# A state-space block with an FP4 feed-forward: the partial state and the output product from rounded halves

## The chip, the cores and the metric

The kernel runs on one core of one Trainium2 chip. The metric is the device time of one execution in microseconds (us); the median of three runs is shown. Five engines work side by side, each through its own instructions in order: TensorE (PE, matrix products and transposes into PSUM), VectorE (DVE), ScalarE (ACT), GpSimd (POOL), and SyncE (SP), which here only issues transfers. They wait for each other on semaphores.

## The reference, cut to what matters

The input is x of 8 x 2048 x 256 in float32. The first half is a simplified Mamba block, the second a feed-forward whose operands are quantised to FP4 in blocks of 16:

```
x_proj, z = split(x @ W_in)                      # 512 + 512 columns
x_conv = silu(causal 4-tap conv(x_proj) + conv_b)
ssm = x_conv @ W_xproj                           # 1 + 16 + 16 columns: delta, B, C
deltaB = softplus(ssm[..., 0]) * B
h_mean = einsum('bld,bln->bdn', x_conv, deltaB) / L      # the state
y = (einsum('bdn,bln->bld', h_mean, C) + D * x_conv) * silu(z)
x = layernorm(x + y @ W_out)                     # the output product
x = layernorm(x + fp4(silu(fp4(x) @ fp4(w_gate).T) * (fp4(x) @ fp4(w_up).T)) @ fp4(w_down).T)
```

## The kernel before, in words

The sequence is cut into 32 groups of 512 positions, four to a batch row. A group has four steps (j = 0 to 3), and a step works on a block of 128 of the 512 inner columns in the first half, and on a tile of 128 positions in the second. All stages run in one software pipeline, whose order is written out by hand for each engine. In one step of the steady part, group g, PE does in this order:

1. gate and up products of an earlier tile (`gate_and_up`, 18 products),
2. the input product of this block (`x_product`), and transposes of an earlier tile's FP4 values (`transposed_h`),
3. `y_product`: the finished state of a batch row times C, for a block five groups back. DVE adds the D term (`skip`, line 1128), POOL multiplies by silu(z) (line 460) into `g`,
4. `output_projection` (line 608): four products of `g` (128 x 128) with `wout` (128 x 256), both float32,
5. only in j = 2: `partial_state` (line 619), four products of `dB` (128 x 48) with `xct` (128 x 512), both float32, summed into bank pc; DVE adds pc into `hacc` (line 1134),
6. `state_projection` and `transposed_conv` of the block before (its transpose goes through bank pa into `xct`, which has two slots, one for each of two groups), `transposed_x`, `z_product`; in j = 3 also `transposed_c` (line 678), which uses bank pa again,
7. `down_projection`, 17 products of 256 columns.

In j = 2 the products of item 6 stand in another order than in the rest (`transposed_x`, `z_product`, `state_projection`, `transposed_conv`).

The other products are made of float32r halves already: a value is rounded to float32r (high), the rest to float32r as well (low), and high x high, high x low and low x high are summed (`split_product`, line 532).

`dB` is made by DVE in `scaled_b`, at the end of step j = 1 (lines 1138 and 1142), so it is ready a step before its use. DVE's order in a steady step is: the sum after the down product (line 1164), codes of x (1001 to 1013), two convolution taps (1104), rounding of x (1019, 1022), `h_product` (1190), `skip` (1128), `h_absmax` (1001), `h_rests` (1199, 1202), `h_scales` (1005, 1009), `attn_sum` (1218), `h_codes` (1013), `add_projection` (1115 or 1119), `x_rests` (1228), `h_round` (1019, 1022; the first waits for ACT's magnitudes, line 898), and in j = 2 at the end the split of the next input (`split_input`, line 1037).

POOL multiplies the values of x (427), gates (460), sums a tap (`conv_sum`, 450), does three small operations of the layer norm (411, 413, 415), and multiplies the codes of h (470, 472). ACT normalises with their result (`r1_rows`, line 904); after that, it makes in j = 0 the softplus (from line 808 on) and in j = 2 the high half of the next input (line 780). DVE's x codes of the next step read what `r1_rows` wrote. ACT's `x_big` (line 867) comes behind the softplus, and DVE's rounding of x waits for it.

The first 24 steps also quantise and transpose the weights; the last 20 have no first half any more.

Of the kernel before, what the change touches and what calls it, by code (L numbers as in the profile page):

```python
# [52 lines left out]
def block_kernel(nc, x, x_t, W_in, conv_w, conv_b, W_xproj, D_skip, W_out, w_gate, w_up, w_down, out):  # L53
# [13 lines left out]
    H3 = 3 * NS  # L67
    LAG = SPS + 1
# [11 lines left out]
    with ExitStack() as ctx:  # L80
# [13 lines left out]
        wout = sb("wout", [P, NB, DM])  # L94
# [11 lines left out]
        ctr = sb("ctr", [H3, SPS, ST], F32R)  # L106
# [9 lines left out]
        xct = sb("xct", [P, 2, TPS, DI])  # L116
# [4 lines left out]
        ccat = sb("ccat", [P, TPS, H3])  # L121
        hacc = sb("hacc", [H3, DI])
        hcat = sb("hcat", [H3, DI], F32R)

        g = sb("g", [P, 2, NB, ST])
# [58 lines left out]
        xct_copied = sem("xct_copied")  # L184
        ssm_pe = sem("ssm_pe")
# [16 lines left out]
        yd_done = sem("yd_done")  # L202
        g_ready = sem("g_ready")
        xres_landed = [sem("xres_landed0"), sem("xres_landed1")]
# [37 lines left out]
        scratch = sb("scratch", [P, 5 * GW + 2 * FF + KM * P])  # L242
        flat_g = g[:, :, :, :].rearrange("p a b c -> p (a b c)")
        raw_g = scratch[:, 0:GW]
        raw_u = flat_g[:, GW + 9 * (GW // QB):2 * GW + 9 * (GW // QB)]
        raw_d = scratch[:, 5 * GW:5 * GW + 2 * FF]
        twice_d = scratch[:, 5 * GW + 2 * FF:5 * GW + 2 * FF + KM * P]
        quant_w = [scratch[:, n * GW:(n + 1) * GW] for n in range(1, 4)]
        w_big = [scratch[:, 4 * GW:5 * GW], flat_g[:, 0:GW], raw_g]

        at = [0]

        def over_scratch(width):

            at[0] += width
            assert at[0] <= scratch.shape[1]
            return scratch[:, at[0] - width:at[0]]

# [8 lines left out]
        GQ = GW // QB  # L267
        w_small = [[flat_g[:, GW + (3 * n + r) * GQ:GW + (3 * n + r + 1) * GQ] for r in range(3)]
                   for n in range(3)]
# [45 lines left out]

        def conv_bank(g_):

            return pgu[:, 1024:1536] if g_ <= LAG else pa[:, :]

# [7 lines left out]
        def _(q):  # L327
# [19 lines left out]
            def body(g_, s, b):  # L347
                i = g_ - LAG
                for j in range(TPS):
# [6 lines left out]
                    if exists(w + 1):  # L356

                        n, half = (j + 1) % 2, 16 * (2 * i + (j + 1) // 2 + 1)
                        wait_apart(q, (xc_saved[n], half), (sz_saved[n], half), (g_ready, w))
                        q.dma_start(xl[:, n, :], xc_hbm[w + 1]).then_inc(xl_landed[n], 16)  # L360
                        q.dma_start(zl[:, n, :], sz_hbm[w + 1]).then_inc(zl_landed[n], 16)
# [22 lines left out]
        def _(pool):  # L384
# [33 lines left out]
            def body(g_, s, b):  # L418
                i = g_ - LAG
                for j in range(TPS):  # L420
# [35 lines left out]
                    if p2 and g_ <= NSUP:  # L456
# [3 lines left out]
                        pool.tensor_tensor(g[:, second(s) % 2, j, :], g[:, second(s) % 2, j, :], zl[:, j % 2, :],  # L460
                                           ALU.mult).then_inc(g_ready, 1)
                    if p1 and g_ > LAG:
                        conv_sum()
                    if exists(to) and g_ <= NSUP:
                        layer_norm(to, ssq1_done, r1_ready, rs1_eps, rs1_done, nm1_done, sum1, ssq1, rs1, nm1)
                    if exists(tg):
# [6 lines left out]
                                           spread(qsh[:, :, 1]), ALU.mult).then_inc(hprod_done, 1)  # L473
                    if j == 0 and exists(v):
# [3 lines left out]
                        c2 = ccat[:, :, :].rearrange("p t (a n) -> p t a n", a=3)  # L478
                        pool.tensor_copy(c2[:, :, 0, :].bitcast(F32R), c_in)
                        pool.tensor_copy(c2[:, :, 2, :].bitcast(F32R), c_in).then_inc(cc_hi, 1)  # L480
# [32 lines left out]
        def _(pe):  # L513
# [40 lines left out]

            def x_product(j, g_, u, v):
# [5 lines left out]
                if g_ > LAG:  # L561
                    at_least(pe, xct_copied, v)
# [13 lines left out]
            def y_product(j, s, b, g_, v, w):  # L576

                wait_apart(pe, (h_ready, b - 1 if s == 0 else b), (ct_ready, g_ - LAG + 1), (g_ready if g_ > NSUP else yd_done, w),
                           (ssm_added, capped(v, NT)))
                if j == 3 and g_ == LAG:  # L580
                    pe.wait_ge(h_added, g_)
# [13 lines left out]
            def output_projection(j, s, i, g_, to, tz):  # L595
# [8 lines left out]
                if i == 1 and j == 0:  # L604
                    pe.wait_ge(w_landed, 32)
                    pe.wait_ge(ct_ready, LAG)
                for c in range(NB):
                    mm = pe.matmul(bank[:, 0:DM], g[:, (second(s) + 1) % 2, c, j * P:(j + 1) * P],  # L608
                                   wout[:, c, :], start=(c == 0), stop=(c == NB - 1))
                mm.then_inc(o_pe, 1)  # L610

            def partial_state(n, added, w):
# [5 lines left out]
                for t in range(TPS):  # L618
                    mm = pe.matmul(pc[0:H3, :], dB[:, t, :], xct[:, (n - 1) % 2, t, :],
                                   start=(t == 0), stop=(t == TPS - 1))  # L620
                mm.then_inc(h_pe, 1)

            def state_projection(j, jb, g_, v, w):
# [6 lines left out]
                elif LAG - 1 <= g_ <= LAG and j == 3 or g_ > LAG and j == 2:  # L630
# [8 lines left out]
            def transposed_conv(g_, jb, u, v):  # L639

                pe.wait_ge(xc_ready, v + 1)
                if g_ <= LAG:
                    at_least(pe, xct_copied, v)
# [26 lines left out]
            def transposed_c(g_, v):  # L670
# [3 lines left out]
                else:  # L674
                    wait_apart(pe, (cc_ready, g_), (xct_copied, capped(v + 1, NT)))
                bank = c_bank(g_)
                for t in range(TPS):
                    mm = pe.transpose(bank[0:H3, t * P:(t + 1) * P], ccat[:, t, :], ident[:, :])
# [20 lines left out]
            def body(g_, s, b):  # L699
                i = g_ - LAG  # L700
                tail = exists(g_ - 1, NSUP)
                for j in range(TPS):
# [3 lines left out]
                    if g_ <= LAG:  # L706
# [5 lines left out]
                        if j == 1 and 2 <= g_ < LAG:  # L712
                            partial_state(g_ - 1, v, w)
                        if exists(v):
                            state_projection(j, jb, g_, v, w)
                            transposed_conv(g_, jb, u, v)
                        if j == 2 and LAG - 1 <= g_:
# [4 lines left out]
                    if g_ > NSUP:  # L722
# [4 lines left out]
                        if exists(td):  # L727
                            transposed_h(td, u)
                        if exists(to):
                            output_projection(j, s, i, g_, to, tz)  # L730
                        if p2:
                            skip_product(j, i, w)
# [17 lines left out]
                    if j == 2 and tail:  # L750
# [614 lines left out]
```

## Time and profile before

| | us |
|---|---|
| median of three runs (1985.72 to 1989.41) | 1985.98 |
| the profiled execution, whole | 1988.75 |
| its span, first to last instruction | 1987.0 |
| PE busy in the span | 1920.3 (97%) |
| DVE busy | 1578.8 (79%) |
| ACT busy | 1265.9 (64%) |
| POOL busy | 1102.5 (55%) |

The granted TensorE clock is 0.986 of full speed in the mean. An engine's busy time says how full it is, not whether the others wait for it. The records of successive products of PE overlap, so what a product costs is read from the distance between starts. Offsets into a step are counted from the start of its first gate product; in one steady group the steps j = 1, 2, 3, 0 start at 998.76, 1012.34, 1029.63 and 1043.62 us, and the next at 1057.20.

### The profile page before, as it was taken

Reading aid. Unit: us, or ns where it says so; the run is one execution under the profiler, and the core shown is the slowest. Engines: PE = TensorE matmul, PEld = TensorE weight load, DVE = VectorE, ACT = ScalarE, POOL = GpSimd, SP = SyncE. Lnnn points to the kernel's source line nnn. Section 1 sums busy time; section 2 is a strip of 40 time slices with the busy share of each in tenths; the row PEclk is TensorE's granted clock in tenths of the full one; section 3 lists DMA queues with packets and bytes.
Section 4 is the critical chain, followed back from the end, with each engine's and each line's share of the span. In section 5 each row is a group of like instructions: output and inputs, shape, how many; then the busy total and the mean of one; then the engine's idle time right before and its main releaser. Section 6 shows DMA issues by size and latency. Waiting matters only on the chain. (4 is left out here: it accounts for less than half of the span.)

```text
span 1987.0 us, 34279 instructions
## 1 busy us (share of the span) xinstructions
PE 1920.3 (97%) x10180; PEld 1540.1 (78%) x10180; DVE 1578.8 (79%) x3549; ACT 1265.9 (64%) x2617; POOL 1102.5 (55%) x1758
## 2 busy tenths in 40 slices
PE   6898999999999999999999999999999999999996
PEld 5665788888878888888788788888888888777775
DVE  5645788878888888888888888888788887788885
ACT  6776666666666666666666666666666666544443
POOL 3434555556555656655556665565565556555553
PEclk8898999999999999999999999999999999999998
DMA  5234233232322322323223232232323223222210
GB/s 167 96 122 144 91 100 103 89 109 99 102 100 98 99 95 99 109 94 109 96 85 107 99 109 96 99 104 88 109 99 101 100 88 99 69 65 73 72 38 16
DMA packets 120309, 190.60 MB, mean 96 GB/s; under 512 B 15040, under 2 KB 49728, under 8 KB 120128
## 3 DMA queue, kind: packets, MB, share of 16 engines
q1 hardware_dynamic: 120128, 188.42, 28.5%
q8 instruction: 85, 1.39, 0.3%
q14 instruction: 96, 0.79, 0.1%
HBM read 104.48 MB, written 83.89 MB: 95 GB/s over the span
## 5 line engine op out<-in xcount | busy, mean ns | idle before, releaser
L532 PE MATMUL pgu<-wgu_hi,xqT 128*128 128x512 f32 (+1 forms) x1536 | 427.1, 386 | 7.6 <-issue 6.5
L532 PEld LDWEIGHTS pgu<-wgu_hi,xqT 128*128 128x128 f32 x1536 | 278.7, 189 | 72.0 <-issue 9.9
L532 PE MATMUL pd<-wd_hi,hqT 128*128 128x256 f32 (+1 forms) x1536 | 315.9, 297 | 5.2 <-issue 2.1
L532 PEld LDWEIGHTS pd<-wd_hi,hqT 128*128 128x128 f32 (+1 forms) x1536 | 247.7, 190 | 26.6 <-issue 4.8
L1019 DVE SCALAR_TENSOR_TENSOR scratch<-scratch 128x256 f32<-128x256 f32 (+2 forms) x258 | 171.8, 666 | 96.7 <-ACT scratch L898 77.4
L411 POOL TENSOR_SCALAR rs<-ssq 128x1 f32<-128x1 f32 x256 | 72.4, 283 | 310.3 <-issue 297.3
L532 PE MATMUL pgu<-wgu_lo,xqT 128*128 128x512 f32 (+1 forms) x768 | 228.0, 378 | 0.0
L1104 DVE SCALAR_TENSOR_TENSOR acc<-xps,cw,acc 128x512 f32<-128x512 f32 x256 | 200.3, 782 | 30.8 <-POOL acc L450 26.2
L608 PE MATMUL pd<-wout,g 128*128 128x256 f32 x864 | 215.4, 392 | 0.0
L802 ACT ACTIVATE scratch<-scratch,sum 128x256 f32<-128x256 f32 x256 | 130.2, 509 | 123.4 <-DVE scratch L1164 118.4
L472 POOL TENSOR_TENSOR scratch<-hnq,qsh 128x704 f32<-128x704 bf16 x128 | 188.7, 1474 | 0.0
L608 PEld LDWEIGHTS pd<-wout,g 128*128 128x128 f32 x864 | 155.2, 189 | 42.6 <-issue 25.8
L413 POOL TENSOR_TENSOR rs<-rs,nhalf 128x1 f32<-128x1 f32 x256 | 170.4, 666 | 21.6
L532 PE MATMUL pd<-wd_lo,hqT 128*128 128x256 f32 x640 | 181.6, 284 | 0.0
L872 ACT ACTIVATE scratch<-pgu 128x704 f32<-128x704 f32 x128 | 96.6, 755 | 116.5 <-PE pgu L532 116.5
L450 POOL TENSOR_TENSOR acc<-acc,tap 128x512 f32<-128x512 f32 x128 | 164.3, 1284 | 11.4 <-ACT tap L846 11.4
L635 PEld LDWEIGHTS pc<-wxp,xcs 128*128 128x128 f32 x1024 | 134.6, 194 | 38.5 <-ACT xcs L829 21.6
L460 POOL TENSOR_TENSOR g<-g,early 128x512 f32<-128x512 f32 x112 | 143.1, 1278 | 35.5 <-DVE g L1128 35.2
L532 PEld LDWEIGHTS pgu<-wgu_lo,xqT 128*128 128x128 f32 x768 | 143.2, 189 | 23.5
L415 POOL TENSOR_SCALAR nm<-sum,rs 128x1 f32<-128x1 f32 x256 | 131.4, 513 | 43.8 <-POOL rs L413 43.8
L635 PE MATMUL pc<-wxp,xcs 128*128 128x33 f32 x1024 | 128.7, 271 | 24.6 <-ACT xcs L829 17.5
L427 POOL TENSOR_TENSOR scratch<-xnq,qsx 128x256 f32<-128x256 bf16 x128 | 81.3, 635 | 118.6 <-DVE xnq L1022 115.5
(140 smaller groups left out, 4489.8 us busy)
## 6 DMA issues: line engine op xcount, KB each, us to landing
sz_hbm<-szs SPq DMA_DIRECT2D x128, 256.0 KB, 2.0
xc_hbm<-xcs SPq DMA_DIRECT2D x128, 256.0 KB, 2.0
early<-xc_hbm SPq DMA_DIRECT2D x128, 256.0 KB, 2.7
early<-sz_hbm SPq DMA_DIRECT2D x128, 256.0 KB, 3.0
xin<-in_x_t_dram SPq DMA_DIRECT2D x32, 512.0 KB, 4.7
xres<-in_L_attn_x_dram SPq DMA_DIRECT2D x128, 128.0 KB, 2.4
out_dram<-scratch SPq DMA_DIRECT2D x128, 128.0 KB, 1.7
early<-in_L_attn_W_in_dram SPq DMA_DIRECT2D x2, 512.0 KB, 4.7
```

What stands on the lines that cost most here:

```text
L413: pool.tensor_tensor(rs[:, :], rs[:, :], nhalf[:, :], ALU.pow).then_inc(rs_done, 1)
L415: pool.tensor_scalar(nm[:, :], total[:, :], rs[:, :], -1.0 / DM, ALU.mult, ALU.mult)\
L450: pool.tensor_tensor(acc[:, j % 2, :], acc[:, j % 2, :], tap0[:, j % 2, :], ALU.add).then_inc(tap_done, 1)
L460: pool.tensor_tensor(g[:, second(s) % 2, j, :], g[:, second(s) % 2, j, :], zl[:, j % 2, :], ALU.mult).then_inc(g_ready, 1)
L472: pool.tensor_tensor(blocks(hq[:, 0:FF]), blocks(hnq[:, :]), spread(qsh[:, :, 1]), ALU.mult).then_inc(hprod_done, 1)
L532: mm = pe.matmul(bank, lhsT, rhs, start=(m == 0), stop=(m == len(pairs) - 1))
L608: mm = pe.matmul(bank[:, 0:DM], g[:, (second(s) + 1) % 2, c, j * P:(j + 1) * P], wout[:, c, :], start=(c == 0), stop=(c == NB - 1))
L635: mm = pe.matmul(pc[:, t * NX:(t + 1) * NX], xcs[:, jb % 2, t * P:(t + 1) * P], wxp[:, jb, :], start=True, stop=True)
L802: act.activation(dev[:, 0 if ssq is ssq1 else 1, :], r, ACT.Square, bias=total[:, :], scale=-1.0 * DM, accum_out=ssq[:, :]).then_inc(ssq_d ...
L872: act.activation(hbuf[:, 0:FF], pgu[:, 0:FF], ACT.Silu).then_inc(sg_ready, 1)
L1019: return dve.scalar_tensor_tensor(v, big, HALF_STEP, v, ALU.max, ALU.add)
L1104: dve.scalar_tensor_tensor(acc[:, jb % 2, :], xps[:, jb % 2, k:k + ST], cw[:, jb, k:k + 1], acc[:, jb % 2, :], ALU.mult, ALU.add).then_inc ...
```

## The change

The output product of a tile is made from halves: `g` becomes `g_hi` and `g_lo`, `wout` becomes `wo_hi` and `wo_lo`, all float32r, and four float32 products become twelve float32r ones. To make them, the gated block goes to a new pair `gx`; ACT rounds it (`gate_high`), and POOL takes the rest (`gate_rest`), one more operation of 128 x 512 on each.

The partial state of a group, for groups 1 and 4 and up counted from 0, is made from halves as well: `xct` now holds the high and the low half of one group in place of two groups; DVE makes the low half (`conv_rest`, 128 x 512, from bank pa). `dB` becomes `dBr` of 80 columns (three copies, a pad of zeros, the low half), by three operations in place of one. Four float32 products become eight float32r ones. Since `xct` has room for one group only, `partial_state` moves from step j = 2 to step j = 1, behind the output product; `scaled_b` moves to just behind `h_absmax` of the same step. `transposed_c` and the next `x_product`, which write bank pa, now wait for `conv_rest` too. The startup splits `wout`, and its scratch space is laid out anew.

```diff
+                pairs = []
                 for c in range(NB):
-                    mm = pe.matmul(bank[:, 0:DM], g[:, (second(s) + 1) % 2, c, j * P:(j + 1) * P],
-                                   wout[:, c, :], start=(c == 0), stop=(c == NB - 1))
-                mm.then_inc(o_pe, 1)
+                    high, low = gated_tile(g_hi, i - 1, c, j), gated_tile(g_lo, i - 1, c, j)
+                    pairs += [(high, wo_hi[:, c, :]), (high, wo_lo[:, c, :]), (low, wo_hi[:, c, :])]
+                split_product(bank[:, 0:DM], DM, pairs).then_inc(o_pe, 1)
...
-                for t in range(TPS):
-                    mm = pe.matmul(pc[0:H3, :], dB[:, t, :], xct[:, (n - 1) % 2, t, :],
-                                   start=(t == 0), stop=(t == TPS - 1))
+                if split_state(n - 1):
+                    pe.wait_ge(xct_rest, split_blocks(4 * n))
+                    pe.matmul(pc[0:HR, :], dBr[:, 0, :], xct[:, 0, 0, :], start=True, stop=False)
+                    for t in range(TPS):
+                        pe.matmul(pc[0:H3, :], dBr[:, t, 0:H3], xct[:, 1, t, :], start=False, stop=False)
+                    for t in range(1, TPS):
+                        mm = pe.matmul(pc[0:HR, :], dBr[:, t, :], xct[:, 0, t, :], start=False, stop=(t == TPS - 1))
...
-                    wait_apart(pe, (cc_ready, g_), (xct_copied, capped(v + 1, NT)))
+                    wait_apart(pe, (cc_ready, g_))
+                    transposed_free(capped(v + 1, NT))
...
-                    if j == 2 and tail:
+                    if j == 1 and tail:
                         partial_state(g_, v, w)
-                    if j != 2 and exists(v):
+                    if j != 1 and exists(v):
                         state_projection(j, jb, g_, v, w)
                         transposed_conv(g_, jb, u, v)
...
+                    def gate_high():
+                        act.wait_ge(gate_done, w + 1)
+                        at_least(act, o_pe, 4 * (i - 1) + j + 1)
+                        act.activation(gated_block(g_hi, i, j), tiles_of(gx[:, j % 2, :]), ACT.Copy).then_inc(g_high, 1)
...
+                    def gate_rest():
+                        pool.wait_ge(g_high, w + 1)
+                        pool.tensor_tensor(gated_block(g_lo, i, j), tiles_of(gx[:, j % 2, :]),
+                                           gated_block(g_hi, i, j), ALU.subtract).then_inc(g_ready, 1)
                     if p1 and g_ > LAG:
                         conv_sum()
+                    if p2 and g_ <= NSUP:
+                        gate_rest()
...
+                        dve.tensor_tensor(dBr[:, :, 0:H3].rearrange("p t (a n) -> p t a n", a=3), *thrice,
+                                          ALU.mult).then_inc(dB_high, 1)
+                        dve.tensor_tensor(dBx[:, :, :], b_in, delta[:, :].unsqueeze(2).broadcast_to([P, TPS, NS]),
+                                          ALU.mult).then_inc(dB_exact, 1)
+                        dve.wait_ge(dB_high, n)
+                        dve.wait_ge(dB_exact, n)
+                        dve.tensor_tensor(dBr[:, :, HL:HR], dBx[:, :, :], dBr[:, :, 0:NS],
+                                          ALU.subtract).then_inc(dB_ready, 1)
...
+                    def conv_rest():
+                        if not split_state(v // TPS):
+                            return
+                        view = conv_bank(g_).rearrange("p (t n) -> p t n", t=TPS)
+                        dve.wait_ge(xct_copied, v + 1)
+                        dve.tensor_tensor(xct[:, 1, :, jb * P:(jb + 1) * P], view,
+                                          xct[:, 0, :, jb * P:(jb + 1) * P], ALU.subtract).then_inc(xct_rest, 1)
...
                     if exists(tg):
                         h_absmax()
+                    if j == 1 and tail:
+                        scaled_b()
                     if exists(td):
                         h_rests()
...
                     if exists(tx):
                         x_rests()
+                    if j != 1 and exists(v):
+                        conv_rest()
```

## Rows read from the trace of the kernel before

**Rows 1.** Windows of steps j = 1, 2, 3, 0: engines' busy us (records), clock.

```profile
998.76:1012.34 13.58, 13.58 (x78) 11.57 (x77) 11.28 (x27) 11.61 (x24) 9.38 (x16) 1.00 0.29 98
1012.34:1029.63 17.29, 17.29 (x86) 12.34 (x85) 13.01 (x31) 9.58 (x20) 9.73 (x15) 1.00 0.30 98
1029.63:1043.62 13.99, 13.99 (x81) 11.88 (x80) 12.75 (x29) 9.11 (x20) 6.52 (x13) 1.00 0.22 79
1043.62:1057.20 13.58, 13.58 (x77) 11.58 (x76) 12.09 (x29) 8.61 (x18) 8.69 (x13) 1.00 0.37 128
```

**Rows 2.** Timeline of PE in that group: start us, length of the merged records, count.

```profile
1010.02 0.28 PE L532 MATMUL pd<-wd_hi,hqT 128*128 128x256 f32 x1
...
1011.70 0.71 PE L532 MATMUL pd<-wd_hi,hqT 128*128 128x256 f32 x3
...
1013.38 1.10 PE L532 MATMUL pgu<-wgu_hi,xqT 128*128 128x512 f32 x4
1014.32 0.63 PE L532 MATMUL pgu<-wgu_lo,xqT 128*128 128x512 f32 x2
...
1018.87 1.99 PE L608 MATMUL pd<-wout,g 128*128 128x256 f32 x8
1020.79 3.63 PE L619 MATMUL pc<-xct,dB 128*48 128x512 f32 x8
...
1040.87 0.60 PE L678 MATMUL pa<-ident,ccat 128*48 128x128 f32 x4
```

**Rows 3.** Timeline of DVE in step j = 1, which starts at 998.76.

```profile
1005.40 0.75 DVE L1128 SCALAR_TENSOR_TENSOR g<-early,dsk,pc 128x512 f32<-128x512 f32 x1 [0.62 <-PE pc L583]
...
1006.86 0.68 DVE L1199 TENSOR_TENSOR hqT<-pe_,hqT 128x512 fp32r<-128x512 f32 x1
...
1008.67 0.89 DVE L1013 SCALAR_TENSOR_TENSOR scratch<-scratch,qsh 128x704 f32<-128x704 f32 x1
...
1010.67 0.89 DVE L1019 SCALAR_TENSOR_TENSOR scratch<-scratch 128x704 f32<-128x704 f32 x1 [0.59 <-ACT scratch L898]
...
1012.48 0.16 DVE L1138 SCALAR_TENSOR_TENSOR delta<-ssm,sp 128x4 f32<-128x4 f32 x1
1012.67 0.48 DVE L1142 TENSOR_TENSOR dB<-ssm,delta 128x192 f32<-128x192 f32 x1
```

**Rows 4.** Timeline of POOL and ACT in the same step.

```profile
998.77 1.28 ACT L808 ACT_TABLE_LOAD   x1
...
1002.66 0.40 ACT L867 ACTIVATE scratch<-scratch 128x256 f32<-128x256 f32 x1
...
1006.23 1.28 POOL L460 TENSOR_TENSOR g<-g,early 128x512 f32<-128x512 f32 x1 [0.29 <-DVE g L1128]
...
1007.46 1.29 POOL L450 TENSOR_TENSOR acc<-acc,tap 128x512 f32<-128x512 f32 x1
...
1010.12 0.19 POOL L411 TENSOR_SCALAR rs<-ssq 128x1 f32<-128x1 f32 x1 [1.36 <-issue]
...
1011.73 0.60 ACT L904 ACTIVATE scratch<-scratch,nm,rs 128x256 f32<-128x256 f32 x1 [0.60 <-POOL nm L415]
```

**Rows 5.** Timeline from the end of step j = 2 into step j = 3.

```profile
1028.00 0.59 ACT L904 ACTIVATE scratch<-scratch,nm,rs 128x256 f32<-128x256 f32 x1
...
1028.65 1.42 POOL L472 TENSOR_TENSOR scratch<-hnq,qsh 128x704 f32<-128x704 bf16 x1
...
1029.22 2.00 DVE L1037 TENSOR_TENSOR xt_lo<-xin,xt_hi 128x512 fp32r<-128x512 f32 x2 [0.71 <-ACT xt_hi L780]
...
1036.24 0.75 DVE L1128 SCALAR_TENSOR_TENSOR g<-early,dsk,pc 128x512 f32<-128x512 f32 x1 [0.18 <-PE pc L583]
```

**Rows 6.** Timeline of the startup, around a long operation of POOL.

```profile
52.54 2.81 POOL L398 TENSOR_TENSOR scratch<-scratch,g 128x1536 f32<-128x1536 f32 x1
...
52.62 4.07 DVE L1104 SCALAR_TENSOR_TENSOR acc<-xps,cw,acc 128x512 f32<-128x512 f32 x2 [1.86 <-POOL acc L450]
...
57.40 1.92 PE L635 MATMUL pc<-wxp,xcs 128*128 128x33 f32 x8 [3.74 <-ACT xcs L829]
```

More of the change, by code:

```diff
@@ L67, in block_kernel @@
     H3 = 3 * NS
+    HR = H3 + 2 * NS
+    HL = H3 + NS
     LAG = SPS + 1
@@ L120, in block_kernel @@
         dB = sb("dB", [P, TPS, H3])
[L121 to L125, printed above, removed]
+        dBr = sb("dBr", [P, TPS, HR], F32R)
+        dBx = sb("dBx", [P, TPS, NS])
+        ccat = sb("ccat", [P, TPS, HR])
+        hacc = sb("hacc", [HR, DI])
+        hcat = sb("hcat", [HR, DI], F32R)
+        g_hi = sb("g_hi", [P, NB, TPS, P], F32R)
+        g_lo = sb("g_lo", [P, NB, TPS, P], F32R)
         xres = sb("xres", [P, 2, DM])
@@ L257, in over_scratch, with tiles_of, gated_block, gated_tile @@
             return scratch[:, at[0] - width:at[0]]
+        raw_g, raw_u, raw_d = from_scratch(GW), from_scratch(GW), from_scratch(2 * FF)
+        quant_w = [raw_g, raw_u, raw_d]
+        twice_d = from_scratch(KM * P)
+        BIG = at[0]
+        w_big = [from_scratch(GW), from_scratch(GW)]
+        w_big.append(w_big[0])
+        GQ = GW // QB
+        w_small = [[from_scratch(GQ) for r in range(3)] for n in range(3)]
+        wout = from_scratch(NB * DM).rearrange("p (c d) -> p c d", c=NB)
+        def tiles_of(ap):
+            return ap.rearrange("p (t n) -> p t n", t=TPS)
+        def gated_block(half, i, c):
+            return half[:, c, :, :] if i % 2 == 0 else half[:, :, c, :]
+        def gated_tile(half, i, c, t):
+            return half[:, c, t, :] if i % 2 == 0 else half[:, t, c, :]
+        later = [0]
+        def over_scratch(width):
+            later[0] += width
+            assert later[0] <= scratch.shape[1]
+            return scratch[:, later[0] - width:later[0]]
         hbuf = over_scratch(2 * FF)
@@ L473, in body @@
                                            spread(qsh[:, :, 1]), ALU.mult).then_inc(hprod_done, 1)
+                    if p2 and g_ > NSUP:
+                        gate_rest()
                     if j == 0 and exists(v):
@@ L933, in body @@
                         weight_copies(u)
+                        if u == 17:
+                            act.wait_ge(w_landed, 32)
+                            act.activation(wo_hi[:, :, :], wout, ACT.Copy).then_inc(wo_h, 1)
                         if exists(v):
                             conv_copy()
+                        if exists(w):
+                            gate_high()
                         if j == 2:
@@ L1320, in body @@
                         x_rests()
+                    if j != 1 and exists(v):
+                        conv_rest()
                     if exists(tg):
                         h_round()
-                    if j == 2 and exists(v):
+                    if j == 1 and exists(v):
                         add_projection()
-                    if j == 1 and tail:
-                        scaled_b()
+                    if j == 1 and exists(v):
+                        conv_rest()
                     if j == 3 and s == 0 and tail:
```

147 lines of the change are left out of this document (95 added, 52 removed).

## The prediction, made before the changed kernel had run

> **What bounds the kernel now.** I read first the page's list of busy times, then the wait list of PE, then the windows of one steady group step by step, and last the timeline of every engine in these steps. In the windows PE is busy for the whole of each step, at a granted clock of 1.00, which is the 2.4 GHz level [rows 1]. DVE works 11.3 to 13.0 us of a step and POOL 6.5 to 9.7. So in the steady part, some 26 whole groups of 13.58 + 17.29 + 13.99 + 13.58 = 58.44 us, PE is the bound, and the others have room. What the reader should look for is how much room: at which offset of a step each result is made, and at which offset PE asks for it. A saving on PE makes it ask earlier.
>
> **What PE saves.** The output product is 8 records (a float32 product is two) in 1.92 us, up to the next product [rows 2]. The new one is twelve float32r products of 256 columns, the shape of the down product, where 14 starts take 1011.70 - 1010.02 = 1.68, or 0.12 each [rows 2]. That is 1.44 us, so 0.4 saved a step (a little of the 1.92 is a switch to 48 columns that stays). The partial state takes 3.6 us: 3.63 in its row [rows 2], and its step is 3.71 longer than a plain one [rows 1]. The new one is eight float32r products of 512 columns, whose starts lie (1014.32 - 1013.38)/4 = 0.235 apart [rows 2]: 1.9, with a switch 2.0 (bounds 1.9 and 2.4, for more switches between 48 and 80 columns). It saves 1.6. A group saves 4 x 0.4 + 1.6 = 3.2 us, if PE never waits. The steps would be 13.2 long, and the one with the partial state 15.2.
>
> **What is added elsewhere.** In each step ACT gets a copy of 128 x 512 (0.6, as its like), POOL `gate_rest` (1.28, the shape of lines 460 and 450 [rows 4]), DVE `conv_rest` (0.68, the shape of line 1199 [rows 3]). `scaled_b` grows by two operations of 128 x 64: the operation on 192 elements took 0.48, that on 4 took 0.16 [rows 3], so some 0.22 each. Busy time allows all this. I cost the copy at nothing: ACT stands idle for 0.60 before line 904 alone [rows 4]. The extra cast of `ccat` and 80 columns for 48 in hcat and ctr I also cost at nothing (bounds 0 and 0.3 a group).
>
> **First new wait: dB, in j = 1.** `dB` was made at the end of this step and used in the next. Now PE wants it behind the output product. That starts 6.53 into a step (1018.87 - 1012.34), so PE arrives at 6.53 + 1.44 = 7.97. DVE can't start `skip` before `y_product` is done, at 6.64 (1005.40), and it had 0.62 of idle there [rows 3]. Behind it comes `h_absmax`, and the next operation starts at 8.10 (1006.86). There `scaled_b` begins: delta 0.19, the 192 elements 0.3 to 0.48, two small ones 0.22 each, with waits between them. It is ready at 9.2. PE waits for 1.2 at least. Behind PE's wait stands the rest of its step.
>
> **Second new wait: bank pa, in j = 3.** PE wants to write pa for `transposed_c` at 1040.87 - 1029.63 = 11.24, now 0.4 earlier, at 10.84. `conv_rest` has to be done first, and it stands behind `x_rests` in DVE. That ends where the idle 0.59 before line 1019 begins, 11.32 into the step [rows 3], so `conv_rest` ends at 12.0 when `skip` starts at 6.64, that is 5.35 behind the start of `skip`. PE waits for 1.2. But in this step `skip` starts later. The split of the next input, at the end of j = 2, comes 1.2 behind `r1_rows` (1028.00 to 1029.22 [rows 5]). In the long step of before it was done 1.6 into j = 3, and DVE still had 0.18 idle before `skip` [rows 5], so `skip` comes 4.85 behind it at the earliest. Now that step is 4.1 shorter. `r1_rows` starts at 12.97 (1011.73 [rows 4]), the split at 14.2 and, with 0.68 for each of its two operations, it ends at 15.5, 2.3 into j = 3. `skip` follows at 7.15, `conv_rest` ends at 12.5, and PE waits for 1.7.
>
> **POOL against DVE.** While POOL worked on line 398 from 52.54 to 55.35, two taps of DVE took 4.07 [rows 6]; 256 of them average 0.78. While line 472 ran until 1030.07, the two operations of the split took 2.00, which is 0.85 of waiting and 1.15 of work [rows 5]. Both DVE operations read two operands from SBUF. So I take such a DVE operation and a large POOL operation to exclude each other. The Trainium skill (SBUF — State Buffer, section "Who interferes with whom") states just this: a DVE instruction with two SBUF inputs and a GpSimd instruction that reads SBUF share one port pair, and the first holds it to its end. By that rule the trace agrees, with the 4.07 above, and the change comes out slower; without it, near the time of before.
>
> What it does here: `gate_rest` is issued when line 450 ends, at 9.94, just behind the start of line 1013 at 9.91 [rows 3, 4]. It waits for that to end and is done at some 11.95, where the three small operations began at 11.36 [rows 4]. These then meet both operations of `h_round`, and I put `r1_rows` 1.0 later, at 13.95 (bounds 0 and 2). In j = 0 the softplus stands behind it. Its start, at 0.01 of j = 1 [rows 4], moves by 1.0 and by the 0.4 of the shorter step, and with it `x_big`, from 3.90 to 5.3. `skip` was possible 2.12 behind `x_big` (1005.40 - 0.62 - 1002.66), so it now comes at 7.42. Then delta is due at 8.88, the large product of `scaled_b` at 9.07. It reads two SBUF operands and meets the gating of POOL, which started 0.83 behind `skip` and lasts 1.28, to 9.5. The last operation has to wait for a semaphore, and in that gap line 450 takes its turn, 1.2 more. dB is ready at 11.2 in place of 9.2.
>
> In j = 2 the split starts at 15.15, meets line 472 until 15.7, ends at 16.85, that is 3.65 into j = 3; `skip` 8.5, `conv_rest` 13.85, PE goes on at 13.9.
>
> **The sum.** j = 1: 11.2 + 2.0 + what follows the partial state, 17.29 - 8.45 - 3.6 = 5.24, gives 18.45. j = 2: 13.2. j = 3: 13.9 + (13.99 - 11.24) = 16.65. j = 0: 13.2. Together 61.5, 3.05 more than 58.44; in 26 groups +79. In the startup two partial states save 1.6 each, against the halves of wout; its steps wait on a loop over ACT, POOL and DVE. In the last 20 steps PE waits for DVE, and a faster output product gives nothing. I take both at 0 (bounds -8 and +12). 1988.75 + 79 = 2068 for a profiled execution. That one was 2.8 above the median of the runs, so 2065.
>
> **The rivals.**
>
> A, the forecast, both waits widened by POOL: 2065, 2035 to 2095.
>
> B, the two waits, but POOL and DVE hardly in each other's way (the small operations slip in between). j = 1 is 9.2 + 2.0 + 5.24 = 16.45, j = 3 is 12.55 + 2.75 = 15.3. With 13.2 twice that is 58.15, -0.3 a group: 1978. With a third of A's delay it is some 2005. For it: in most rows the two engines' durations are steady. Against it: [rows 5, 6].
>
> C, PE stays the bound. It ends on the other side. 3.2 x 26 = 83, and up to 8 in the startup: 1895 to 1903. For it speaks PE's full window [rows 1]. It needs dB at 7.97 and pa free at 10.84. It decides as soon as the two results come more than 1.2 earlier than worked out, and nothing in [rows 3] gives that. Half of it, one wait gone, is 1945.
>
> D, the clock falls in j = 1. There PE would idle for 3.2 us. Behind the idle 3.74 in the startup, 8 records took 1.92 [rows 6], about twice what they take in the steady steps, so the engine ran at 1.2 GHz. If that comes in each group it costs some 3 us more, another 78: 2143. Against it: the wait is shorter than that one.
>
> E, the change doesn't do what it says, and the new products cost as much as the old: then PE saves nothing, waits 3.2 less a group in j = 1 and j = 3, and the time is A's or above. I fold it into D.
>
> **How the numbers follow.** Chances: A 0.50, B 0.24, C 0.14 with its half, D and E 0.12. What a measurement can tell from no change is 0.2%, 4 us. B lies on both sides of it: 0.06 faster, 0.04 same, 0.14 slower. So faster 0.20, same 0.04, slower 0.76. The range for 8 in 10 takes in A and B and a bit of D: 1972 to 2105. A's own is 2035 to 2095.
>
> **What the profile of after would show.** Right: idle time of PE before the new partial state released by DVE's dBr, of 1.2 to 3.3 us in each group, and before `transposed_c` released by DVE's xct, of 1.2 to 3; twelve products in 1.44; a steady group of 61 to 62 us with j = 1 and j = 3 long and j = 0 and j = 2 at 13.2; `gate_rest` or its neighbours on POOL longer than 1.28, and ACT line of `r1_rows` near 14 into the step. Wrong: PE without idle time and a group of 55 us (C), or small waits only (B). The step most likely to fail is the 1.0 of delay of `r1_rows`, since it hangs on which of two operations 0.03 us apart comes first.

## The result, and the profile after

The changed kernel takes 2195.51 us (median of four runs, 2194.39 to 2196.32); the kernel before, beside it, 1987.7. The ratio is 1.1046 [1.1029, 1.1064]: 10% slower. I had forecast 2065 and a range up to 2105. Both new waits are there. The one for `dB` is 5.55 us long where the sum had 3.2 (11.2 - 7.97), and two costs stand beside them that the sum didn't have: a slow clock, and a wait for `skip` in j = 3.

First the windows of a steady group, in the page's order of columns (us; busy of PE, PEld, DVE, ACT, POOL; clock; DMA share; GB/s), steps j = 3, 0, 1, 2, to be held against [rows 1]:

```profile
1004.79:1022.06 17.27, 15.18 (x86) 13.23 (x85) 13.64 (x30) 10.85 (x23) 12.75 (x18) 0.90 0.28 95
1022.06:1034.91 12.85, 12.85 (x82) 11.42 (x81) 11.04 (x27) 8.94 (x19) 9.47 (x13) 1.00 0.38 120
1034.91:1057.48 22.57, 17.02 (x89) 13.67 (x88) 16.64 (x33) 12.72 (x26) 13.09 (x22) 0.85 0.24 82
1057.48:1070.36 12.88, 12.88 (x82) 11.45 (x81) 10.98 (x27) 8.51 (x18) 8.36 (x12) 1.00 0.18 63
```

The group takes 65.57 us, 7.1 more than before. The trace has 25 such groups, 100 steps from the first steady j = 1 on (248.82 to 1892.66, before 238.95 to 1698.20). They take 1643.8 us in place of 1459.2, 185 of the 206 that the span grew by; the startup ahead of them takes 9.9 more, and the 25 steps behind them 11.1. The even steps last 12.85 and 12.88, 0.7 less than a plain step before (13.58), and PE is busy throughout: there the change does what it says. In j = 1 PE is idle for 5.55, and its clock is no longer whole: 0.85 of full speed in the mean of the window is a part of it at 1.2 GHz and the rest at 2.4. In j = 3 it is idle for 2.09, at 0.90.

The list of PE's waits says who ends them (us in total, times, the longest):

```profile
PE pc L687 <- DVE dBr L1258: 150.5, 28, 5.9
PE pc L710 <- issue: 58.2, 27, 4.4
PE pa L754 <- DVE xct L1266: 14.3, 12, 1.2
```

L687 is the first product of the partial state, L710 `state_projection`, L754 `transposed_c`. The first is the wait for `dB` that was forecast. The third is the wait for bank pa, of which the sum had 3.1 a group (13.9 - 10.84); the list has little of it, and what became of it is told with the reasons. The second was not forecast.

This is PE's timeline in j = 1 (start, length, count; idle time before it and its releaser in brackets), to hold against [rows 2]:

```profile
1041.16 0.28 PE L593 MATMUL pd<-wo_hi,g_hi 128*128 128x256 f32 x1
...
1042.45 0.28 PE L593 MATMUL pd<-wo_hi,g_lo 128*128 128x256 f32 x1
...
1048.28 0.72 PE L687 MATMUL pc<-xct,dBr 128*80 128x512 f32 x1 [5.55 <-DVE dBr L1258]
1048.80 1.91 PE L689 MATMUL pc<-xct,dBr 128*48 128x512 f32 x4
1050.50 1.48 PE L691 MATMUL pc<-xct,dBr 128*80 128x512 f32 x3
1052.06 1.04 PE L593 MATMUL pb<-xt_hi,win_hi 128*128 128x512 f32 x2
```

The twelve output products start 0.117 apart, 1.4 in all, as worked out. The partial state runs from 1048.28 to the next product at 1052.06, 3.78 where 2.0 was forecast: it stands behind the idle 5.55 and runs at half speed.

DVE and POOL in the same step show why `dB` comes so late, to hold against [rows 3, 4]:

```profile
1043.00 0.74 DVE L1227 SCALAR_TENSOR_TENSOR scratch<-early,dsk,pc 128x512 f32<-128x512 f32 x1
1043.99 1.27 POOL L508 TENSOR_TENSOR scratch<-scratch,early 128x512 f32<-128x512 f32 x1
1044.45 0.82 DVE L1238 SCALAR_TENSOR_TENSOR delta<-ssm,sp 128x4 f32<-128x4 f32 x1
1045.21 1.27 POOL L498 TENSOR_TENSOR acc<-acc,tap 128x512 f32<-128x512 f32 x1
1045.31 1.39 DVE L1252 TENSOR_TENSOR dBr<-ssm,delta 128x192 fp32r<-128x192 f32 x1
1046.44 1.37 POOL L513 TENSOR_TENSOR g_lo<-scratch,g_hi 128x512 fp32r<-128x512 f32 x1
1046.62 1.28 DVE L1254 TENSOR_TENSOR dBx<-ssm,delta 128x64 f32<-128x64 f32 x1
1048.00 0.23 DVE L1258 TENSOR_TENSOR dBr<-dBx,dBr 128x64 fp32r<-128x64 f32 x1
```

POOL has three large operations in a row: gating, `conv_sum`, `gate_rest`. DVE has a chain of small ones, and each of the first three ends only when the POOL operation beside it has ended: 0.82 for four elements (0.16 before), 1.39 for 192 (0.48 before), 1.28 for 64. Over the whole trace the operation on 64 elements has a median of 1278 ns, so this is so in most groups and not this group's luck.

### The profile page after: what moved, and what is told of

Same layout as the page of the kernel before. It is cut to its first block and busy times, and to the rows that moved or that the text cites. A ratio compares the mean times of both kernels' runs of the same rounds, so it can differ in the third digit from the quotient of the medians.

```text
span 2192.6 us, 35927 instructions
## 1 busy us (share of the span) xinstructions
PE 1886.4 (86%) x10692; PEld 1594.0 (73%) x10692; DVE 1724.5 (79%) x3725; ACT 1337.1 (61%) x2746; POOL 1351.0 (62%) x1919
## 5 line engine op out<-in xcount | busy, mean ns | idle before, releaser
L593 PE MATMUL pgu<-wgu_hi,xqT 128*128 128x512 f32 (+1 forms) x1536 | 425.8, 385 | 12.3 <-issue 11.1
L459 POOL TENSOR_SCALAR rs<-ssq 128x1 f32<-128x1 f32 x256 | 101.2, 395 | 319.0 <-issue 301.2
L513 POOL TENSOR_TENSOR g_lo<-scratch,g_hi 128x512 fp32r<-128x512 f32 x128 | 222.5, 1738 | 8.1 <-ACT g_hi L956 8.1
L1117 DVE SCALAR_TENSOR_TENSOR scratch<-scratch 128x704 f32<-128x704 f32 (+2 forms) x259 | 172.9, 667 | 67.6 <-ACT scratch L951 34.1
L461 POOL TENSOR_TENSOR rs<-rs,nhalf 128x1 f32<-128x1 f32 x256 | 212.5, 830 | 21.3
L710 PE MATMUL pc<-wxp,xcs 128*128 128x33 f32 x1024 | 140.5, 284 | 80.5 <-issue 58.2
L710 PEld LDWEIGHTS pc<-wxp,xcs 128*128 128x128 f32 x1024 | 137.9, 206 | 95.7 <-issue 68.7
L993 ACT ACTIVATE scratch<-scratch,nm,rs 128x256 f32<-128x256 f32 x128 | 76.7, 599 | 177.9 <-POOL nm L463 177.9
L528 POOL TENSOR_TENSOR scratch<-hnq,qsh 128x704 f32<-128x704 bf16 x128 | 183.6, 1434 | 0.0
L982 ACT ACTIVATE xqT<-pe_ 128x256 fp32r<-128x256 f32 x128 | 48.7, 380 | 188.5 <-PE pe_ L733 188.5
L494 POOL COPY hist<-xps 128x3 f32<-128x3 f32 x128 | 27.5, 215 | 215.2 <-ACT acc L920 215.2
```

Source lines behind the costliest of these rows:

```text
L459: pool.tensor_scalar(rs[:, :], ssq[:, :], 1.0 / DM ** 3, EPS, ALU.mult, ALU.add).then_inc(eps_done, 1)
L461: pool.tensor_tensor(rs[:, :], rs[:, :], nhalf[:, :], ALU.pow).then_inc(rs_done, 1)
L513: pool.tensor_tensor(gated_block(g_lo, i, j), tiles_of(gx[:, j % 2, :]), gated_block(g_hi, i, j), ALU.subtract).then_inc(g_ready, 1)
L528: pool.tensor_tensor(blocks(hq[:, 0:FF]), blocks(hnq[:, :]), spread(qsh[:, :, 1]), ALU.mult).then_inc(hprod_done, 1)
L593: mm = pe.matmul(bank, lhsT, rhs, start=(m == 0), stop=(m == len(pairs) - 1))
L710: mm = pe.matmul(pc[:, t * NX:(t + 1) * NX], xcs[:, jb % 2, t * P:(t + 1) * P], wxp[:, jb, :], start=True, stop=True)
```

## The experiments

Unless said otherwise an experiment is an edit of the changed kernel. All ratios are to the kernel before on the same chip.

### The place of scaled_b, and the clock

```diff
# e1_early_db: DVE, j = 1
 tap(1)
 tap(2)
+if j == 1 and tail: scaled_b()
...
 h_absmax()
-if j == 1 and tail: scaled_b()
# e2_filler: PE, partial_state; the wait for dB stands behind the other waits and the fillers
-pe.wait_ge(dB_ready, n)
...
+if n > LAG:
+    for t in range(20):
+        pe.matmul(pc[:, :], wgu_hi[:, 0, 0:P], wgu_hi[:, 1, 0:512], start=True, stop=True)
+pe.wait_ge(dB_ready, n)
```

> The changed kernel, but in step j = 1 the four small operations that make dB stand behind the two taps of DVE, some 5 us earlier, where DVE idles for ACT and POOL has little to do. Theory (the wait of PE for dB, made long by POOL's three large operations in a row, costs the group its time, and the slow clock comes behind that wait): PE no longer waits in j = 1, that step falls from 22.6 to 15 to 16 us, the clock stays high behind it, and the kernel takes 1995 to 2035 us. Rival (another engine sets the length of the group and the wait for dB only shows it): the wait moves to another product and the kernel stays above 2120 us.

> The changed kernel with 20 idle products of 512 columns (4.7 us) on PE ahead of its wait for dB, in each steady group; their sums are overwritten and nothing else is changed. The wait itself stays. Theory (the pause lets the clock fall to 1.2 GHz for the partial state behind it): no slow records behind the wait in j = 1, partial state 2.0 in place of 3.8 us, 1.8 to 2.2 us less a group, 2130 to 2150 us. Rival (the products of the new form are slow by themselves): 2190 to 2200 us, the partial state still 3.8 us.

e1: 2053.03 us, ratio 1.0331 [1.0304, 1.0358]. 142 us come back, so the place of `scaled_b` beside POOL's three operations is most of the loss, though 18 are left above what was expected. DVE and POOL, a step j = 1 that starts at 1032.29:

```profile
1037.45 0.15 DVE L1238 SCALAR_TENSOR_TENSOR delta<-ssm,sp 128x4 f32<-128x4 f32 x1
1037.64 0.36 DVE L1252 TENSOR_TENSOR dBr<-ssm,delta 128x192 fp32r<-128x192 f32 x1
1037.91 0.22 DVE L1254 TENSOR_TENSOR dBx<-ssm,delta 128x64 f32<-128x64 f32 x1
1038.24 0.23 DVE L1258 TENSOR_TENSOR dBr<-dBx,dBr 128x64 fp32r<-128x64 f32 x1
...
1041.38 0.43 PE L687 MATMUL pc<-xct,dBr 128*80 128x512 f32 x1 [1.27 <-DVE scratch L1227]
```

Where POOL has nothing large, the same four operations take 1.0 from start to end in place of 3.8. PE now waits at L687 for `skip`, 1.27: the next wait in the queue behind the one removed.

e2: 2150.98 us, 1.0814 [1.0798, 1.083], 1 us above its range. The twenty products compute nothing that is used and keep PE at work while `dB` is made. PE's timeline:

```profile
1027.70 4.81 PE L686 MATMUL pc<-wgu_hi 128*128 128x512 f32 x20 [1.15 <-DVE scratch L1230]
1032.35 0.40 PE L690 MATMUL pc<-xct,dBr 128*80 128x512 f32 x1
...
1034.33 0.71 PE L593 MATMUL pb<-xt_hi,win_hi 128*128 128x512 f32 x2
```

The partial state takes 1.98 (1032.35 to 1034.33) in place of 3.78, and the kernel gets 44.5 us faster by doing more work. The step j = 1 lasts 20.67 in place of 22.57, at a granted clock of 1.00 in place of 0.85, and `dB` is ready no earlier (1032.13, 13.40 into the step): 1.9 a group is the price of the fallen clock in j = 1, shown. It comes on top of the wait.

### Which half of the change costs

```diff
# e4_state_only: g and wout stay float32, four float32 products in the output product; gate_high and gate_rest are gone
-split_product(bank[:, 0:DM], DM, pairs).then_inc(o_pe, 1)
+pe.matmul(bank[:, 0:DM], g[...], wout[:, c, :], ...)
# e3_output_only: no group is split, partial_state and scaled_b stand where they stood before
 def split_state(k):
-    return k == 1 or k >= LAG - 1
+    return False
# e5_no_gate_rest: g_lo stays zero
-pool.tensor_tensor(gated_block(g_lo, i, j), ...).then_inc(g_ready, 1)
+pool.memset(idle[:, :], 0.0).then_inc(g_ready, 1)
```

> The partial state from halves alone; the output product is as before, with float32 operands, and so without the added operations of ACT and POOL. Theory: both new waits (dB, and bank pa in j = 3) stay, narrower as without gate_rest, and the output product costs 0.4 us a step more than in the changed kernel: 2070 to 2130 us, all of it slower than before. Rival (the output product is what costs): at or below 1986 us.

> The output product from halves alone, with the added copy of ACT and gate_rest of POOL; the partial state is as before: float32 operands, two slots of xct, in step j = 2, dB at the end of step j = 1 (dB's and C's rows keep their 80 columns). Theory (the two new waits belong to the partial state; the delay of r1_rows by gate_rest is 1 to 1.5 us, and only its way over the softplus costs PE a little): PE saves 0.4 us a step, and loses up to 0.5 a group: 1940 to 1975 us, faster than before. Rival (gate_rest alone pushes DVE and PE out of step): above 2000 us.

> The changed kernel with POOL's gate_rest left out: one element is set in its place, and the low half of the gated block stays zero, so that the output product lacks its share. Theory (POOL's added 1.28 us and its exclusion with DVE's operations on two SBUF operands widen both waits): dB is ready some 2 us earlier in j = 1, r1_rows comes 1 to 2 us earlier, the lag in j = 3 shrinks by 1, together 3.5 to 5 us a group: 2065 to 2110 us. Rival (only the order of DVE counts, not POOL): within 1% of 2195 us.

e4: 2069.2, 1.0412 [1.0394, 1.0429], 1 us below its range. e5: 2073.09, 1.0426 [1.0411, 1.0442], inside it. The two agree: without the third POOL operation PE waits for `dB` 69.4 us in all in e4 and 80.7 in e5, about half of the 150.5. The partial state's halves alone cost 82 us. In e4 the forecast second wait does stand in the list of PE's waits, at nearly the size of the bare one (1.2):

```profile
PE pa L746 <- DVE xct L1249: 30.6, 26, 1.2
```

e3: 1985.52, 0.9981 [0.9971, 0.9992]. It was expected between 1940 and 1975, or above 2000 by the rival; it is neither. The products are cheaper, and nothing comes of it. The 25 groups take 1446.1 us for 1459.2, 13 less, and the startup with 2.7 more and the last 25 steps with 9.6 more (298.4 for 288.8) take that back. What the groups lack goes in step j = 1, as PE and DVE show:

```profile
1002.24 0.74 DVE L1225 SCALAR_TENSOR_TENSOR scratch<-early,dsk,pc 128x512 f32<-128x512 f32 x1
...
1003.08 1.05 PE L710 MATMUL pc<-wxp,xcs 128*128 128x33 f32 x8 [1.09 <-issue]
```

`skip` ends at 1002.98, and `state_projection`, which writes the bank that `skip` reads, starts 0.10 later. The trace names "issue" as the releaser, but the code has a wait on `yd_done` there, and the distance is the same in each case that I read: skip ends at 1010.40 and L710 starts at 1010.50 in a step j = 3 of e1; in the changed kernel's j = 3 it is 1014.60 and 1014.71:

```profile
1013.86 0.74 DVE L1227 SCALAR_TENSOR_TENSOR scratch<-early,dsk,pc 128x512 f32<-128x512 f32 x1
...
1014.71 1.39 PE L710 MATMUL pc<-wxp,xcs 128*128 128x33 f32 x8 [2.09 <-issue]
...
1018.47 0.68 DVE L1266 TENSOR_TENSOR xct<-pa,xct 128x512 fp32r<-128x512 f32 x1
...
1019.30 0.61 PE L754 MATMUL pa<-ident,ccat 128*80 128x128 f32 x4
```

So I read the 58.2 us of "issue" as a wait for `skip`. Before, `skip` of j = 1 ended at 7.4 into the step (1005.40 + 0.75 - 998.76) and PE came at 8.4, a cover of one microsecond. In e3 PE comes at 7.8 (8.91 less the idle 1.09) and `skip` ends at 8.81 (1002.98 - 994.17). In 8 of 24 groups slow products follow this short wait: the step j = 1 then lasts 16.0 in place of 14.5, at a granted clock of 0.89 (529.44 to 545.45). That `skip` comes later through `gate_rest` on POOL is borne out by e11 below, where only the place of `gate_rest` differs and the list of waits has 7.8 us of "issue" in place of 32.9.

### Taking the waits away one by one

Each of these has the edit of the one before it too, and starts from e1.

```diff
# e6_late_gate_rest: POOL, steady steps
-gate_rest()            # behind conv_sum
 layer_norm(...)
 h_codes_product(...)
+gate_rest()
# e7_early_split: ACT, j = 2
+split_input(g_ + 1)
 r1_rows()
-split_input(g_ + 1)
# e8_late_transposed_c: PE, j = 3; ACT's c_copy behind r1_rows
-transposed_c(g_, v)
 down_projection(g_, to, td)
+transposed_c(g_, v)
# e10_next_step_rest: POOL
 x_values()
+if p2 and j > 0 and g_ <= NSUP:
+    gate_rest(w - 1, j - 1)
...
-if p2:
-    gate_rest()
+if p2 and (j == 3 or g_ > NSUP):
+    gate_rest(w, j)
```

> As e1_early_db, and gate_rest stands behind the layer norm and the codes of h in POOL's order. Its result is needed only in the next group. Theory (in its old place gate_rest holds back the layer norm, r1_rows, and through it softplus, x_big and the split of the input; the skip that PE waits for in j = 1 and j = 3 is late by that): r1_rows starts near 13 us into a step in place of 14.4, the wait ahead of the partial state goes, the one in j = 3 falls below 1 us and with it the slow records, 1945 to 1990 us. Rival (POOL's total work counts, not its place): within 1% of the 2053 us of e1_early_db.

> As e6_late_gate_rest, and in step j = 2 ACT makes the high half of the next input ahead of r1_rows, in the time in which it waits for POOL, so that DVE can split the input about 1 us earlier. Theory (the rest of the wait in j = 3 comes from this split, since the step in which it stands is 4 us shorter than it was): another 0.5 to 1.5 us a group, 1915 to 1970 us. Rival (r1_rows alone was the cause): same as e6_late_gate_rest within 0.3%.

> As e7_early_split, and in step j = 3 transposed_c stands behind the down product in PE's order, its copy behind r1_rows in ACT's, so that PE doesn't stand still for conv_rest. Theory (the wait for bank pa is 1 us or more in each group): 0.8 to 1.5 us a group less, 1890 to 1945 us, PE's full saving. Rival (that wait is small once the lag is gone): within 0.5% of e7_early_split.

> As e8_late_transposed_c, but gate_rest of a block stands in the next step, between the values of x and the gating, where DVE works on one SBUF operand (the last block of a group keeps its place). Theory (in e8_late_transposed_c gate_rest excludes the two taps of DVE, 2.60 us in place of 1.53, and the skip of j = 1 is late by it): taps back at 1.53, the wait ahead of the partial state 0 to 0.5 in place of 1.05, 1935 to 1965 us. Rival (the skip of j = 1 is late because of the softplus alone): within 0.3% of 1970 us.

| | us | ratio |
|---|---|---|
| e1 | 2053.03 | 1.0331 [1.0304, 1.0358] |
| e6 | 2014.1 | 1.0128 [1.0113, 1.0143] |
| e7 | 1998.36 | 1.005 [1.0035, 1.0065] |
| e8 | 1970.44 | 0.9906 [0.9891, 0.9921] |
| e10 | 1938.08 | 0.9744 [0.9728, 0.9759] |

e6, e7 and e8 all ended above their ranges. e6 gave 39 us where at least 63 were expected; e7 (15.7, or 0.6 a group) and e8 (27.9, or 1.1 a group) gave steps of the size expected from a worse start. Each time I had taken away a wait and missed the next. In e8 it stood in DVE's and POOL's timeline of j = 1:

```profile
1046.63 1.48 POOL L513 TENSOR_TENSOR g_lo<-scratch,g_hi 128x512 fp32r<-128x512 f32 x1
1046.89 2.60 DVE L1201 SCALAR_TENSOR_TENSOR acc<-xps,cw,acc 128x512 f32<-128x512 f32 x2
...
1053.10 0.42 PE L685 MATMUL pc<-xct,dBr 128*80 128x512 f32 x1 [1.05 <-DVE scratch L1225]
```

Behind the codes of h, `gate_rest` runs into the next step and shuts out DVE's two taps: 2.60 where e1 has 1.53 (1036.00 in its trace). DVE comes 1.07 later, `skip` with it, and PE waits for 1.05. e10 puts `gate_rest` in between the x values and the gating, in the place where DVE reads PSUM or one operand, and there it takes its bare time and hurts nobody; POOL, DVE and PE in j = 1 of e10:

```profile
1032.64 0.74 DVE L1227 SCALAR_TENSOR_TENSOR scratch<-early,dsk,pc 128x512 f32<-128x512 f32 x1
1032.74 1.28 POOL L480 TENSOR_TENSOR g_lo<-scratch,g_hi 128x512 fp32r<-128x512 f32 x1
...
1033.30 0.88 DVE L1099 TENSOR_REDUCE qsh<-scratch 128x44 f32<-128x704 f32 x1
...
1033.64 0.43 PE L687 MATMUL pc<-xct,dBr 128*80 128x512 f32 x1
```

The partial state has no idle time before it any more. `skip` reads PSUM and `h_absmax` one operand, and neither is longer for the POOL operation beside it.

### Is the place of gate_rest enough, and is the partial state worth it?

```diff
# e12_rest_alone: the changed kernel itself; e11_output_next_rest: the same edit in e3
-gate_rest()            # behind conv_sum
...
 x_values()
+if p2 and j > 0 and g_ <= NSUP:
+    gate_rest(w - 1, j - 1)
# e9_output_late_rest: e3 with e6's edit
-gate_rest()            # behind conv_sum
 layer_norm(...)
 h_codes_product(...)
+gate_rest()
```

> The changed kernel, with gate_rest of a block in the next step as in e10_next_step_rest and nothing else changed: dB is still made where the change put it. Theory (gate_rest costs by its place, and the wait for dB costs by its own): the same gain as with gate_rest left out, 2055 to 2090 us, and a wait for dB of some 3 us that is still there. Rival (e5_no_gate_rest gained by less work of POOL): above 2120 us.

> As e3_output_only (output product from halves alone), with gate_rest behind the layer norm and the codes of h in POOL's order. Theory (what e3_output_only lacks of its 40 us is the delay of r1_rows by gate_rest, which makes the skip of step j = 1 late): the wait ahead of the state projection in j = 1 goes, 1940 to 1970 us. Rival (the added operations of ACT and POOL cost their time wherever they stand): within 0.4% of 1985 us.

> As e9_output_late_rest, with gate_rest in the next step as in e10_next_step_rest. Theory: POOL's place for it meets no DVE operation on two SBUF operands, so PE gets all of its 0.4 us a step: 1935 to 1955 us. Rival: same as e9_output_late_rest within 0.3%.

e12: 2122.66, 1.0675 [1.0657, 1.0692], a miss, and in the range of the rival (above 2120), by which e5 gained through less work of POOL. DVE, POOL and PE in j = 1:

```profile
1014.10 0.19 DVE L1238 SCALAR_TENSOR_TENSOR delta<-ssm,sp 128x4 f32<-128x4 f32 x1
1014.23 1.27 POOL L515 TENSOR_TENSOR scratch<-scratch,early 128x512 f32<-128x512 f32 x1
1014.32 1.39 DVE L1252 TENSOR_TENSOR dBr<-ssm,delta 128x192 fp32r<-128x192 f32 x1
1015.45 1.38 POOL L505 TENSOR_TENSOR acc<-acc,tap 128x512 f32<-128x512 f32 x1
...
1015.63 1.28 DVE L1254 TENSOR_TENSOR dBx<-ssm,delta 128x64 f32<-128x64 f32 x1
...
1017.29 0.45 PE L687 MATMUL pc<-xct,dBr 128*80 128x512 f32 x1 [3.29 <-DVE dBr L1258]
```

With two large operations in place of three the small ones still lose to each, and only the first (0.19) slips through. `skip` comes at 6.45 into the step in place of 8.09, so its delay came from the place of `gate_rest`; the wait for `dB` stays (95.4 us in 28 times). Behind the idle 3.29 the partial state again runs slow, 3.4 to the next product. Of the 50 us between e12 and e5, 10 lie in the last 25 steps, where `gate_rest` keeps its place in e12 (300.4 for 290.5), so the rival is partly right. For the wait for `dB` it is the place of `scaled_b` that has to change.

e9: 1971.67, 0.9917 [0.9901, 0.9934], just above the expected 1970. e11: 1939.16, 0.975 [0.9735, 0.9764]. e11 has no halves in the partial state and is as fast as e10. The windows say why: first those of e10, steps j = 0 and 1 (j = 2 and 3, left out, last 12.86 and 13.53) and the sum of all four,

```profile
...
1011.79:1025.87 14.08, 13.35 (x84) 11.49 (x81) 13.14 (x31) 9.70 (x21) 10.52 (x14) 1.00 0.40 135
1025.87:1041.84 15.97, 15.11 (x90) 12.45 (x89) 14.57 (x33) 12.47 (x26) 13.13 (x20) 1.00 0.37 117
sum 56.44, PE 54.85 PEld 47.21 DVE 51.73 ACT 40.76 POOL 42.16; mean PE 13.71 PEld 11.80 DVE 12.93 ACT 10.19 POOL 10.54
```

and the sum of four steps (j = 1, 2, 3, 0) of e11:

```profile
sum 56.39, PE 56.08 PEld 47.06 DVE 50.60 ACT 41.20 POOL 39.90; mean PE 14.02 PEld 11.77 DVE 12.65 ACT 10.30 POOL 9.97
```

Both groups last 56.4, and the mean of 24 groups is 55.8 in both. PE is busy for 1.2 less in e10, and idle for 1.6 where e11 idles for 0.3: 0.73 before `state_projection` in j = 0, where `skip` is late again, and 0.86 in j = 1, where it waits until DVE has taken the partial state out of the bank (25.2 us over 30 times in the list of waits). These two groups hold the mean of the state, which comes every fourth time. In the others (55.6 in both) the first of these waits is missing, and the steps j = 3 and j = 0 of e10 are 0.3 longer each without idle time, between `transposed_conv` and `z_product`; what makes them longer is not shown.

## Why the prediction was wrong

**The saving of PE was right, and a little small.** Twelve products took 1.4 (forecast 1.44), the partial state at full clock 1.98 (forecast 2.0, seen in e2). The even steps are 12.85 and 12.88 where 13.2 was forecast. Some 0.3 of this is that `y_product` has 80 rows in place of 48, which the sum had at nothing or as a cost: see the last section.

**The wait for dB was right in kind and mis-sized in its term "dB is ready at 11.2".** That is the step that failed. It became ready at 13.32 (1048.23 - 1034.91), and PE went on at 13.37 (1048.28). 0.67 of the 2.1 is that `skip` came at 8.09 for 7.42. The rest lies behind it: from the start of `skip` to the end of the last small operation the sum had 3.8 (11.2 - 7.42), and it took 5.23. The sum let the small operations meet POOL twice, the large one of them the end of the gating, and the last one line 450, and it had `gate_rest` nowhere in this chain. They met it three times: delta the gating, the 192 elements `conv_sum`, the 64 elements `gate_rest`. The prediction argued from [rows 5, 6] that such a pair excludes each other, and then did not ask who goes first each time when a chain of small DVE operations stands beside a row of large POOL ones. The Trainium skill (SBUF — State Buffer, section "Who interferes with whom") calls the shared port pair an exclusive lock; the 0.82, 1.39 and 1.28 agree with it. This term is 2.2 us a group, some 54 in 25.

**The fall of the clock was a rival, and came together with the forecast.** D put it on top of A's waits, at "some 3 us more" a group and 2143 in all, and held it at 0.12 together with E, since the wait would be shorter than the 3.74 of the startup. The wait became 5.55, and the partial state behind it takes 3.78 against 2.0: 1.8 a group in j = 1, 45 us, and e2 gives back 44.5. The range took in only "a bit of D", and so it ended at 2105. D's own 2143 is short as well, by the term of `dB` above all.

**The wait in j = 3 was right in what ends it, and lacked its first half.** The sum had `conv_rest` done at 13.85 and PE going on at 13.9. `conv_rest` ended at 14.36 (1018.47 + 0.68 - 1004.79) and `transposed_c` started at 14.51 (1019.30), since `skip` came at 9.07 (1013.86) for 8.5. Half of this lag is a slip of the sum: by [rows 5] line 472 starts 0.65 behind `r1_rows` and lasts 1.42, so it ends at 16.0 and not at 15.7. The lag of `skip` is why the step came out at 17.27 for 16.65, only 0.6 off. What the sum did not have is that PE already stops at `state_projection`, 2.09 for `skip`. It had `skip` at 8.5 and PE done with the output product at 7.97, so a wait of some 1.3 could be read from it; I did not ask what PE needs from `skip`. The later wait shrinks by what the earlier one takes, and here the slow products behind the earlier one fill the rest of it. In 11 of 24 groups the granted clock of the step is 1.00, and there PE waits the missing 1.2 before `transposed_c`; the step lasts 17.26 all the same. In 6 of the 24 the slow products last longer than `conv_rest` needs, and the step takes 18.75 to 19.1 (1070.36 to 1089.11: `conv_rest` ends at 14.66, `transposed_c` starts at 15.48).

**The step named as likeliest to fail held.** `r1_rows` came 14.4 into j = 0 (1036.46 - 1022.06) where 13.95 was forecast; the 0.45 may be part of the 0.67 by which `skip` is late.

**The account.** The profiled execution took 2194.39 for 2068, 126 more. The group shown gives 4.1 in j = 1 (2.2 of `dB`, 1.8 of clock, 0.1 behind it), 0.6 in j = 3 and some -0.35 in each even step, 4.07 in all, 102 in 25 groups. The 25 groups together grew by 184.6 where the sum had 79 for 26, so 4 more lie in the groups with the longer j = 3. The startup took 9.9 more and the last 25 steps 11.1 more, both of which the sum had at nothing, with 12 as the upper bound of the two. In the last steps it is `gate_rest`: e5, which leaves it out, takes 290.5 there, the kernel before 288.8 and the changed one 299.9. Of the startup's 9.9, e3 has 2.7 and e4 6.0, so either half of the change has a share in it; which wait it is has not been read.

**The rivals.** B needed small operations that slip in between: e1 shows that they take their bare time only where POOL has nothing large. C needs no waits; e10 and e11 reach 55.8 a group in the mean where it had 55.2. E is refuted by the durations.

## What to carry to other kernels

Before a saving on the bound engine is counted, list everything that it will ask for earlier, with the reserve of each in the trace of before: here `skip` had one microsecond, and in e3 PE came 0.5 earlier and `skip`, with one more POOL operation ahead of `r1_rows`, ended 1.4 later (e3: no gain; e11, the same products with that operation in another place: 2.5%). A chain of small DVE operations doesn't belong beside a row of large POOL ones, and a large POOL operation belongs beside DVE work that reads PSUM or one operand. A wait of PE of several microseconds has to be priced with the slow clock behind it, and not against it; e3 shows slow products behind 1.09 us too, in 8 of 24 groups.

## What the runs showed of the hardware that I had not expected

- A DVE operation on 64 elements with two SBUF operands took 1278 ns in the median beside large POOL operations, 218 ns away from them (e1). In the changed kernel's j = 1 `conv_sum` starts at 1045.21, while DVE's next small operation, which waits for the one before to end at 1045.27, starts at 1045.31. So POOL's takes its turn in each gap of the chain, and n small operations pay for n large ones. Which of the two would win if both were ready at the same time, no row here tells.
- Useless products made the kernel 44.5 us faster (e2), since they keep TensorE at 2.4 GHz while it would wait for 5.5 us (granted clock 1.00 in the step j = 1, 0.85 without them).
- A product with 48 rows costs more around it than one with 80. These are PE's rows in j = 0, first of the kernel before and then of e4, which has 80 rows and the old output product, from the last transposes ahead of `y_product` to the first output product:

```profile
1049.42 0.38 PE L572 MATMUL pb<-ident,scratch 128*128 128x128 f32 x2
1049.73 0.49 PE L583 MATMUL pc<-ctr,hcat 48*128 48x512 f32 x1
1050.16 1.99 PE L608 MATMUL pd<-wout,g 128*128 128x256 f32 x8
```

```profile
1047.49 0.38 PE L633 MATMUL pb<-ident,scratch 128*128 128x128 f32 x2
1047.62 0.48 PE L642 MATMUL pc<-ctr,hcat 80*128 80x512 f32 x1
1047.94 1.89 PE L667 MATMUL pd<-wout,g 128*128 128x256 f32 x8
```

From the first start to the last it is 0.74 with 48 rows and 0.45 with 80, and 0.45 in the changed kernel as well (1027.84 to 1028.29). So it goes with the rows and not with the form of the output product. That is 0.29 a step, by my estimate 29 us in 100 steps, of the 64 that the 25 groups of e11 save (1394.9 for 1459.2): e11 owes nearly half of its gain to the 80 rows of C and the state, which it keeps without needing them, and the rest to the output product.
